# Two graph layers on one core: the relation loop's last two rounds peeled off, and the node arithmetic and h2 scatters of 47 groups placed in front of them

## The chip, the cores and the metric

The kernel runs on one core of a Trainium2 chip. The metric is the time of one execution on the device in microseconds, as the median of several. The engines of the core are TensorE (PE in the profile; PEld is its weight load), VectorE (DVE), ScalarE (ACT), GpSimd (POOL) and SyncE (SP). Each works through its own instruction list, and they meet at semaphores.

## The reference, cut to what matters

There are 6250 nodes with 16 features each, 206250 directed edges, and 230 relations. Two layers follow each other:

```
deg = max(number of edges that end in the node, 1);  h = relu(layernorm(x))
x  = x + L0(h, deg ** -0.5, rel_weight, loop_weight, rel_emb, src, dst, edge_type)
h  = relu(layernorm(x))
x  = x + L1(h, edge_attr, W_msg, b_msg, W_attn, b_attn, src, dst)
```

L0 (the relation layer) takes for each edge the row of its source node times the matrix of its relation, maps it with a tanh of its norm, weights it, and sums over the edges of each destination (`numer`, and the weights in `lamsum`). After the sums comes arithmetic per node: a division, a projection to a ball, an addition of the node's own transformed row, a residual sum (`xnew`), and then layernorm and relu of that, which gives `h` for the next layer, called h2 here. L1 (the edge layer) makes two 16 x 16 matrices for each edge from its 16 attributes, multiplies them with the h2 row of the edge's source, and takes a softmax-weighted sum over the edges of each destination.

## The kernel before

Edges come sorted by destination. The kernel ranks the nodes by their number of edges, largest first, and puts them into GC = 49 groups of 128 (one node in each partition). A round, also called a window, treats up to S = 48 edges of each of the 128 nodes of one group. The first group needs two windows, every other one, so there are 50 rounds, numbered k = 0 to 49; the loops run over pairs of rounds (25 iterations), q = k mod 2 chooses the buffer. The last two rounds, 48 and 49, are those of the last two groups, 47 and 48, which have the fewest edges: round 48 has 24 slots and round 49 has 22.

**Set-up.** All relation products go into a table in HBM (`table`), the nodes are ranked, the plan of the windows is made.

**Relation phase** (loop at L358 on POOL, L1022 on DVE, L669 on ACT). For each round POOL issues one indirect DMA per slot (L354, 128 rows of 16 numbers from `table` into `gath`): 18 in any case, then the indices of the next round (`pair_block`, L349), then the rest. DVE waits until all of the round's gathers have landed (L1033), does the arithmetic of the round (L1034 to L1057, with a Sqrt and a Tanh on ACT), and adds to `numer` and `lamsum` of the group. POOL may start the gathers of round k when DVE has finished round k-2 (`l0_math`, L363). In the same loop DVE turns the edge attributes into rows of 100 bf16 numbers, `split_chunk` (L1003 to L1014), one of 50 chunks in each round; SP writes each chunk to `ef6` in HBM (L281) and then loads the chunk after next into the same buffer (L278). The split of a chunk waits for its data, and for the write of the chunk two before it.

**Between the phases.** After the loop DVE does the node arithmetic for all 49 groups at once (L1071 to L1113): tiles of 128 x 784 numbers, one after another, with three square roots on ACT (L676 to L681), and signals `h2_ready`. POOL has waited meanwhile: it needs `start_ready` from ACT (L698), which comes after ACT's third square root. POOL then fetches the source numbers of the first edge window (`src_block`, L387), the edge rows of that window (`edge_rows`, L391, 128 rows of 4800 numbers), and the source numbers of the second, and writes the h2 rows of the 49 groups to HBM by 49 indirect DMAs (L402). It waits until all of these have landed (`h2_out`, L424).

**Edge phase.** 50 windows again. For each, POOL gathers up to 48 h2 rows per node (L354), TensorE transposes the edge rows (L551) and makes the matrices (L557), and DVE multiplies them with the gathered rows (L1182), takes maxima and products, TensorE sums. The first window's products wait for all of its gathers (L1177).

Work that POOL issues goes into one queue in the order of its instructions.

Of the kernel before, what the change touches and what calls it, by code (L numbers as in the profile page):

```python
# [10 lines left out]
ALU = mybir.AluOpType  # L11
# [18 lines left out]
GSTEP = 64  # L30
MINS = MINH * HALF
# [4 lines left out]
WCH = 512  # L36
# [23 lines left out]
def build(nc, x, src, dst, efeat, etype, relw, loopw, relemb, wmsg, bmsg, wattn, battn, out, scratch):  # L60
# [3 lines left out]
    with ctx:  # L64
# [64 lines left out]
        def col256(j, n=1):  # L129
# [71 lines left out]
                 "bst_ready blk_in tg0 tg1 l0_math n2_ready th_ready hnorm hnorm_out h2_ready h2_out "  # L201
# [11 lines left out]
        def steps(eng):  # L213
            n = eng.value_load(npair[0:1, 0:1], min_val=(GC + 1) // 2, max_val=NW // 2 - 2)
            return n, (2 * n + 2) // WCH + 1
# [82 lines left out]
        def _(pool):  # L298
# [38 lines left out]
            pairs = pool.value_load(npair[0:1, 0:1], min_val=(GC + 1) // 2, max_val=NW // 2 - 2)  # L337
# [18 lines left out]

            pair_block(0, 0)
            with pool.Fori(0, pairs) as i:  # L358
                for q in range(2):
                    k = 2 * i + q  # L360
                    _, ns = window_slots(pool, k)
                    pool.wait_ge(m["blk_in"], 16 * k + 16)
                    pool.wait_ge(m["l0_math"], k + 1)  # L363
                    pool.sem_inc(m["passed"], 1)
                    for b in range(MINS):
                        gather(table_d, blkidx, q, b, 1, tgath)
                    if q:
                        pool.wait_ge(tgath[0], pool.snap(cum[0]) * 16)
                        pool.sem_inc(m["passed"], 1)
                    else:  # L370
                        with pool.If(i > 0):
                            pool.wait_ge(tgath[1], pool.snap(cum[1]) * 16)
                            pool.sem_inc(m["passed"], 1)
                    pair_block(k + 1, 1 - q)
                    with ExitStack() as deeper:
                        for b in range(MINS, S):
                            deeper.enter_context(pool.If(ns > b))
                            gather(table_d, blkidx, q, b, 1, tgath)
                    pool.reg_add(cum[q], cum[q], ns)
            pool.wait_ge(m["blk_in"], pairs * 32 + 16)  # L380
            pool.sem_inc(m["passed"], 1)
# [107 lines left out]
        def _(pe):  # L489
# [43 lines left out]
            pairs, nstep = steps(pe)  # L533
# [93 lines left out]
        def _(act):  # L627
# [40 lines left out]
            pairs = act.value_load(npair[0:1, 0:1], min_val=(GC + 1) // 2, max_val=NW // 2 - 2)  # L668
            with act.Fori(0, pairs) as i:  # L669
                for q in range(2):  # L670
                    k = 2 * i + q
                    act.wait_ge(m["n2_ready"], k + 1)
                    nc.scalar.activation(sl[:, 2, :], sl[:, 1, :], ACT.Sqrt)  # L673
                    nc.scalar.drain()
                    nc.scalar.activation(sl[:, 3, :], sl[:, 2, :], ACT.Tanh, scale=SQC).then_inc(m["th_ready"], 1)
            act.wait_ge(m["hnorm"], 1)  # L676
            nc.scalar.activation(nrm[:, 1, 0:GC], nrm[:, 0, 0:GC], ACT.Sqrt).then_inc(m["hnorm_out"], 1)
            act.wait_ge(m["hnorm"], 2)
            nc.scalar.activation(nrm[:, 1, 0:GC], nrm[:, 0, 0:GC], ACT.Sqrt).then_inc(m["hnorm_out"], 1)
            act.wait_ge(m["hnorm"], 3)  # L680
            nc.scalar.activation(nrm[:, 1, 0:GC], nrm[:, 0, 0:GC], ACT.Sqrt).then_inc(m["hnorm_out"], 1)  # L681
# [73 lines left out]
        def _(dve):  # L755
# [188 lines left out]
            ts(npairf[:], npairf[:], -MAGIC, None, ALU.add)  # L944
# [18 lines left out]
            pairs, nstep = steps(dve)  # L963
# [58 lines left out]
            with dve.Fori(0, pairs) as i:  # L1022
                for q in range(2):
                    k = 2 * i + q
                    G = gath[:, q, :, :]
                    g, ns = window_slots(dve, k)
                    dve.reg_add(cum[q], cum[q], ns)
                    V.tensor_scalar(valid[:, q, :], iotaf[:, 0:S], rem[:, q:q + 1], None, ALU.is_lt)
                    V.drain()
                    dve.wait_ge(m["blk_in"], 16 * k + 16)  # L1030
                    dve.sem_inc(m["passed"], 1)
                    window_start(k + 2, q, m["bst_ready"])
                    dve.wait_ge(tgath[q], dve.snap(cum[q]) * 16)  # L1033
                    tt(sq, G, G, ALU.mult)  # L1034
                    row_sum(sl[:, 0, :], sq)
                    V.tensor_scalar(sl[:, 1, :], sl[:, 0, :], MIN_NORM, None, ALU.max).then_inc(m["n2_ready"], 1)  # L1036
                    dve.wait_ge(m["th_ready"], k + 1)
                    ts(sl[:, 2, :], sl[:, 2, :], SQC, None, ALU.mult)
                    V.reciprocal(sl[:, 4, :], sl[:, 2, :])
                    V.drain()  # L1040
                    tt(sl[:, 3, :], sl[:, 3, :], sl[:, 4, :], ALU.mult)
                    tt(sl[:, 4, :], sl[:, 3, :], sl[:, 3, :], ALU.mult)
                    tt(sl[:, 4, :], sl[:, 4, :], sl[:, 0, :], ALU.mult)
                    ts(sl[:, 4, :], sl[:, 4, :], -CURV, 1.0, ALU.mult, ALU.add)
                    ts(sl[:, 4, :], sl[:, 4, :], EPS, 0.5, ALU.add, ALU.mult)
                    V.reciprocal(sl[:, 5, :], sl[:, 4, :])
                    V.drain()
                    tt(sl[:, 5, :], sl[:, 5, :], valid[:, q, :], ALU.mult)
                    row_sum(lsum[:], sl[:, 5, :])
                    tt(sl[:, 3, :], sl[:, 3, :], sl[:, 5, :], ALU.mult)  # L1050
                    V.tensor_tensor(sq, G, bc(sl[:, 3, :], D), ALU.mult)
                    V.drain().then_inc(m["l0_math"], 1)
                    row_sum(nsum[:], sq.rearrange("p s d -> p d s"))
                    V.tensor_tensor(numer[:, ds(g, 1), :].rearrange("p a d -> p (a d)"),
                                    numer[:, ds(g, 1), :].rearrange("p a d -> p (a d)"), nsum[:], ALU.add)
                    V.tensor_tensor(lamsum[:, ds(g, 1)], lamsum[:, ds(g, 1)], lsum[:], ALU.add)
                    V.drain()  # L1057
# [6 lines left out]
            dve.wait_ge(m["blk_in"], pairs * 32 + 16)  # L1064
            dve.sem_inc(m["passed"], 1)


            A, B, T = gtmp(0), gtmp(1), gtmp(2)
            X0, Y = info[:, 0:GC, 0:D], info[:, 0:GC, D:2 * D]
            n0, n1, n2, n3, n4, n5 = (nrm[:, j, 0:GC] for j in (2, 3, 4, 5, 6, 7))  # L1070
            V.tensor_scalar(nrm[:, 0, 0:GC], deg[:, 0:GC], 1.0, None, ALU.max).then_inc(m["hnorm"], 1)  # L1071
            dve.wait_ge(m["hnorm_out"], 1)
            V.reciprocal(n0, nrm[:, 1, 0:GC])
            V.drain()
            tt(n1, n0, deg[:, 0:GC], ALU.mult)
            ts(n1, n1, EPS, None, ALU.add)
            V.reciprocal(n2, n1)
            V.drain()
            tt(n0, n0, n2, ALU.mult)
            tt(n1, n0, lamsum[:, 0:GC], ALU.mult)  # L1080
            ts(n1, n1, EPS, None, ALU.add)
            V.reciprocal(n2, n1)
            V.drain()
            tt(n0, n0, n2, ALU.mult)
            tt(A, numer[:, 0:GC, :], bc(n0, D), ALU.mult)
            tt(T, A, A, ALU.mult)
            row_sum(n0, T)
            V.tensor_scalar(nrm[:, 0, 0:GC], n0, MIN_NORM, None, ALU.max).then_inc(m["hnorm"], 1)
            dve.wait_ge(m["hnorm_out"], 2)
            V.reciprocal(n1, nrm[:, 1, 0:GC])  # L1090
            V.drain()
            ts(n1, n1, (1.0 - BALL) / SQC, 1.0, ALU.mult, ALU.min)
            tt(A, A, bc(n1, D), ALU.mult)
# [184 lines left out]
```

## Time and profile before

| | us |
|---|---|
| median of 3 runs | 6012.68 |
| lowest and highest of the runs | 6012.58, 6017.94 |
| span of the profiled execution | 6008.9 |
| VectorE busy (58% of the span) | 3466.2 |
| GpSimd busy (69%) | 4164.0 |
| TensorE busy (45%) | 2731.4 |

The profiled execution has no time of its own beside its span; the span runs from its first to its last instruction, and the median of the runs is 3.8 us longer. "Busy" says how long an engine worked, not whether anybody waited for it. The granted clock of TensorE is 0.50 of full speed while it idles in the relation phase and about 0.87 in the edge phase.

### The profile page before, as it was taken

Reading aid. Unit: us, or ns where it says so; the run is one execution under the profiler, and the core shown is the slowest. Engines: PE = TensorE matmul, PEld = TensorE weight load, DVE = VectorE, ACT = ScalarE, POOL = GpSimd, SP = SyncE. Lnnn points to the kernel's source line nnn. Section 1 sums busy time; section 2 is a strip of 40 time slices with the busy share of each in tenths; the row PEclk is TensorE's granted clock in tenths of the full one; section 3 lists DMA queues with packets and bytes.
Section 4 is the critical chain, followed back from the end, with each engine's and each line's share of the span. In section 5 each row is a group of like instructions: output and inputs, shape, how many; then the busy total and the mean of one; then the engine's idle time right before and its main releaser. Section 6 shows DMA issues by size and latency. Waiting matters only on the chain.

```text
span 6008.9 us, 57574 instructions
## 1 busy us (share of the span) xinstructions
PE 2731.4 (45%) x13577; PEld 1934.4 (32%) x13578; DVE 3466.2 (58%) x4171; ACT 1368.7 (23%) x1709; POOL 4164.0 (69%) x3713
## 2 busy tenths in 40 slices
PE   3550000000000000000678787888888888887887
PEld 1110000000000000000455565565565656555665
DVE  8601222222222322341688888888888888888886
ACT  3540000000000000000222233223323333333333
POOL 2326777777777777756476777777777777777774
PEclk6555555555555555555788889888888889888988
DMA  5881111111111111111000000100010101011110
GB/s 148 271 263 31 28 23 27 29 33 31 28 30 34 33 31 36 36 38 22 21 13 21 21 21 21 29 21 21 21 30 21 30 22 30 23 28 30 29 29 19
DMA packets 157959, 251.69 MB, mean 42 GB/s; under 512 B 73726, under 2 KB 130563, under 8 KB 145156
## 3 DMA queue, kind: packets, MB, share of 16 engines
q0 software_dynamic: 126192, 100.10, 8.5%
q1 hardware_dynamic: 31711, 151.31, 7.7%
q8 instruction: 9, 0.15, 0.0%
q14 instruction: 15, 0.12, 0.0%
q10 hardware_dynamic: 32, 0.01, 0.0%
HBM read 113.57 MB, written 136.63 MB: 42 GB/s over the span
## 4 chain that ended last, share of the span: by engine, by line
POOL 29%; PE 21%; issue 16%; DVEq 14%; DVE 12%; DMA 6%; POOLq 1%; ACT 1%; SPq 0%; ACTq 0%
POOL gath L354 28%; PE psS L563 9%; PE psS L568 7%; DVEq L1221 6%; DMA table<-arena 4%; DVE stage L1182 4%; PE psW L557 3%; DVE stage L1224 3%; DVEq L1189 2%; DVEq L1182 1%; DVE arena L1182 1%; DMA gath<-h_dram,hidx 1%; DVEq L1138 1%; PE psW L511 1%; DVEq L1151 1%
## 5 line engine op out<-in xcount | busy, mean ns | idle before, releaser
L354 POOL DMA_INDIRECT gath<-h_dram,hidx x1695 | 2100.0, 1239 | 798.9 <-issue 528.0
L354 POOL DMA_INDIRECT gath<-table,blkidx x1646 | 1641.4, 997 | 507.4 <-issue 504.5
L551 PE MATMUL psT<-identb,stage 128*100 128x128 bf16 x2448 | 225.7, 251 | 2341.4 <-DVEq L1138 2322.7
L568 PE MATMUL psS<-stage,ident 128*128 128x256 f32 x3390 | 926.7, 429 | 162.6 <-DVE stage L1224 161.8
L551 PEld LDWEIGHTS psT<-identb,stage 128*100 128x100 bf16 x2448 | 201.8, 150 | 2381.8 <-DVEq L1138 2280.5
L563 PE MATMUL psS<-arena,ident 128*128 128x256 f32 x3390 | 834.7, 384 | 0.0
L1182 DVE TENSOR_TENSOR arena<-psW,gath 128x768 f32 (+1 forms) x565 | 520.8, 951 | 494.4 <-DMA gath<-h_dram,hidx 363.4
L568 PEld LDWEIGHTS psS<-stage,ident 128*128 128x128 f32 x3390 | 703.5, 215 | 313.8 <-DVE stage L1224 205.1
L782 DVE TENSOR_TENSOR work<-gath 128x768 f32<-128x768 f32 x50 | 48.0, 959 | 1286.5 <-DMA gath<-table,blkidx 1286.5
L557 PE MATMUL psW<-wst,stage 100*128 100x256 bf16 x3390 | 576.8, 291 | 294.5 <-DVE arena L1182 212.2
L563 PEld LDWEIGHTS psS<-arena,ident 128*128 128x128 f32 x3390 | 608.5, 192 | 71.2
L712 ACT ACTIVATE arena<-arena 128x1536 f32<-128x1536 f32 (+1 forms) x294 | 421.4, 1433 | 893.2 <-DVE arena L1211 893.2
L1182 DVE TENSOR_TENSOR stage<-psW,gath 128x768 f32 (+1 forms) x565 | 513.7, 949 | 14.8 <-issue 14.8
L1224 DVE TENSOR_TENSOR stage<-stage,arena (+1 forms) x294 | 498.9, 1697 | 30.4 <-ACT arena L712 4.6
L1211 DVE TENSOR_TENSOR arena<-arena,psT 128x1536 f32 (+2 forms) x294 | 495.0, 1684 | 0.0
L673 ACT ACTIVATE work<-work 128x48 f32<-128x48 f32 x50 | 12.1, 243 | 2066.3 <-DVE work L1036 2066.3
L557 PEld LDWEIGHTS psW<-wst,stage 100*128 100x128 bf16 x3390 | 294.4, 101 | 576.4 <-DVE arena L1182 257.3
L707 ACT ACT_TABLE_LOAD x50 | 64.2, 1283 | 1092.7 <-PE psS L571 1092.7
L1196 DVE TENSOR_TENSOR work<-work,arena 128x1536 f32<-128x1536 f32 x171 | 300.7, 1759 | 15.8
L702 ACT COPY stage<-psT 100x1024 bf16<-100x1024 bf16 x306 | 300.7, 996 | 10.4 <-PE psT L551 10.4
L511 PE MATMUL psW<-stage,work 102*125 102x460 bf16 x400 | 181.6, 606 | 194.2 <-ACT arena L645 162.7
L645 ACT COPY arena<-psW 125x920 f32<-125x920 f32 x200 | 175.3, 927 | 211.3 <-DMA table<-arena 159.2
(227 smaller groups left out, 2394.6 us busy)
## 6 DMA issues: line engine op xcount, KB each, us to landing
table<-arena SPq DMA_DIRECT2D x50, 1610.0 KB
ef<-arena SPq DMA_DIRECT2D x50, 805.7 KB
gath<-h_dram,hidx POOLq DMA_INDIRECT x1695
gath<-table,blkidx POOLq DMA_INDIRECT x1646, 2.3
arena<-in_edge_attr SPq DMA_DIRECT2D x50, 257.8 KB
table<-arena SPq DMA_DIRECT2D x50, 186.9 KB
arena<-first_dram POOLq DMA_DIRECT2D x1, 915.5 KB, 12.0
info<-info_dram POOLq DMA_DIRECT2D x2, 432.0 KB, 11.3
```

Source lines behind the costliest of these rows:

```text
L354: pool.indirect_dma_start(out=gath[:, q, s, :], out_offset=None, in_=rows, in_offset=bass.IndirectOffsetOnAxis(ap=idx[:, q, s:s + 1].bitca ...
L551: last = nc.tensor.transpose(psTb[0:KE, t % 2, j, 0:GP], efs[:, 8 * t + j, :], identb[0:GP, 0:GP])
L557: last = nc.tensor.matmul(psW[0:GP, h % 2, j * IO:(j + 1) * IO], efT[:, q, h * HALF + j, 0:GP], wst[:, c0:c0 + IO], start=True, stop=True)
L563: nc.tensor.matmul(psS[0:GP, 0:IO], ident[0:GP, 0:GP], score[:, q, s, :], start=False, stop=False)
L568: nc.tensor.matmul(psS[0:GP, IO:2 * IO], ident[0:GP, 0:GP], prod[:, c0:c0 + IO], start=False, stop=False)
L702: nc.scalar.copy(efT[:, q, 8 * t:8 * t + 8, 0:GP], psTb[0:KE, t % 2, :, 0:GP]).then_inc(m["efT_sb"], 1)
L712: nc.scalar.activation(v, v, ACT.Exp).then_inc(m["exp_done"], 1)
L1182: V.tensor_tensor(dst_ap.rearrange("p s (i o) -> p s i o", o=D), psW[0:GP, s, 0:HALF * IO].rearrange("p (s i o) -> p s i o", i=D, o=D), bc ...
L1196: V.tensor_tensor(macc, macc, score[:, q, ds(b * BLK, BLK), :], ALU.max).then_inc(m["scored"], 1)
L1211: V.tensor_tensor(blk, blk, mnew.unsqueeze(1).to_broadcast([GP, n, IO]), ALU.subtract).then_inc(m["sub_done"], 1)
L1221: V.drain()
L1224: V.tensor_tensor(pr, pr, score[:, q, ds(b * BLK, n), :].rearrange("p s c -> p (s c)"), ALU.mult).then_inc(m["q_ready"], 1)
```

## The change

The loops of the relation phase run over one pair of rounds less (`rest` instead of `pairs`), and the last two rounds stand behind them as code of their own. On DVE, the two chunks that the last pair would have split are split right after the loop; then the node arithmetic is done for groups 0 to 46 (GE = 47), which signals `h2_early`; then rounds 48 and 49; then the node arithmetic of groups 47 and 48, which signals `h2_ready`. On ACT the square roots go in the same order. On POOL the gathers of rounds 48 and 49 come first as before; then it waits for `h2_early` and issues 47 of the h2 scatters; then come the waits for the last gathers and `start_ready`, the three fetches for the edge phase, the wait for `h2_ready`, and the last two scatters. One `pair_block`, that of a round 50 which nobody used, and the waits for it are gone.

```
-            with pool.Fori(0, pairs) as i:
+            with pool.Fori(0, rest) as i:
                 for q in range(2):
...
+                    table_rows(i, q, False)
+            for q in range(2):
+                table_rows(rest, q, True)
...
-            pool.wait_ge(m["start_ready"], 1)
-            src_block(0)
-            edge_rows(0)
-            pool.wait_ge(m["start_ready"], 2)
-            src_block(1)
-
-            pool.wait_ge(m["h2_ready"], 1)
+            pool.wait_ge(m["h2_early"], 1)
             for c in range(GC):
+                if c == GE:
+                    pool.wait_ge(tgath[1], pool.snap(cum[1]) * 16)
+                    pool.sem_inc(m["passed"], 1)
+                    pool.wait_ge(m["start_ready"], 1)
+                    src_block(0)
+                    edge_rows(0)
+                    pool.wait_ge(m["start_ready"], 2)
+                    src_block(1)
+                    pool.wait_ge(m["h2_ready"], 1)
                 pool.indirect_dma_start(out=h2_d, ...
...
+            with dve.If(rest < ECH // 2):
+                for q in range(2):
+                    dve.wait_ge(m[f"ef6_out{q}"], 16 * (ECH // 2 - 1))
+                    dve.sem_inc(m["passed"], 1)
+                    split_chunk(ECH // 2 - 1, q)
+            nodes(0, GE, 0, m["h2_early"])
+            for q in range(2):
+                relation(rest, q)
+            nodes(GE, GC, 3, m["h2_ready"])
```

`relation` and `nodes` are the bodies that stood in the loop (L1025 to L1057) and behind it (L1068 to L1114), with the range of groups a to b as arguments; the instructions are the same. The loop of the relation phase keeps its split of one chunk in each round, now for rounds 0 to 47.

How the instructions stand. First POOL before, from its last gathers of the relation phase on (`table` is where these read; `srcp` holds the source numbers, `ef` the edge rows, `h_dram` is h2 in HBM; ISA rows are waits and register work):

```order
L354 DMA gath<-table,blkidx 128x16
L375 UNCONDITIONAL_BRANCH
L379 ISA
L358 COMPARE_AND_BRANCH
L380 ISA
L387 DMA blkidx<-srcp,ebst 128x48
L391 DMA stage<-ef,ebst 128x4800
L387 DMA blkidx<-srcp,ebst 128x48
L402 DMA h_dram<-arena,nidx 6251x16 x49
```

POOL with the change, at the same place:

```order
L356 DMA gath<-table,blkidx 128x16
L379 UNCONDITIONAL_BRANCH
L383 REGISTER_ALU
L415 DMA h_dram<-arena,nidx 6251x16 x47
L407 ISA
L397 DMA blkidx<-srcp,ebst 128x48
L401 DMA stage<-ef,ebst 128x4800
L397 DMA blkidx<-srcp,ebst 128x48
L415 DMA h_dram<-arena,nidx 6251x16 x2
```

The three fetches stood between the last gather and all 49 scatters; now 47 scatters stand in front of them and 2 behind.

DVE before, at the end of the relation loop (the four rows on `arena` are the split of a chunk, the rows on `nrm` the start of the node arithmetic):

```order
L1006 CAST arena<-arena 125x33x48
L782 TENSOR_TENSOR arena<-arena 125x528
L1010 CAST arena<-arena 125x33x32
L1013 TENSOR_TENSOR arena<-arena 125x33x16
L1058 UNCONDITIONAL_BRANCH
L1022 REGISTER_ALU
L1022 COMPARE_AND_BRANCH
L1064 ISA
L1071 TENSOR_SCALAR nrm<-info 128x49
L1073 RECIPROCAL nrm<-nrm 128x49
L782 TENSOR_TENSOR nrm<-nrm,info 128x49
```

DVE with the change, behind the loop:

```order
L1025 CAST arena<-arena 125x33x48
L801 TENSOR_TENSOR arena<-arena 125x528
L1029 CAST arena<-arena 125x33x32
L1032 TENSOR_TENSOR arena<-arena 125x33x16
L1025 CAST arena<-arena 125x33x48
L801 TENSOR_TENSOR arena<-arena 125x528
L1029 CAST arena<-arena 125x33x32
L1032 TENSOR_TENSOR arena<-arena 125x33x16
L1135 UNCONDITIONAL_BRANCH
L1081 TENSOR_SCALAR nrm<-info 128x47
L1083 RECIPROCAL nrm<-nrm 128x47
```

The loop's end has moved ahead of two splits, and the node arithmetic behind them has 47 columns; the 49-column arithmetic is gone, and rounds 48 and 49 come later, behind the 47 columns.

## Rows read from the trace of the kernel before

**Rows 1.** The page's chain that ended last, shares by engine.

```profile
POOL 29%; PE 21%; issue 16%; DVEq 14%; DVE 12%; DMA 6%; POOLq 1%; ACT 1%; SPq 0%; ACTq 0%
```

**Rows 2.** Windows by phase: us, busy (x instructions) by engine, PEclk, DMA share, GB/s.

```profile
457.00:2686.00 2229.00, 0.00 (x0) 0.00 (x0) 574.50 (x1301) 152.57 (x200) 1689.67 (x1697) 0.50 0.13 31
...
2848.00:6009.00 3161.00, 2525.39 (x13008) 1855.58 (x13008) 2624.34 (x2561) 1011.27 (x1260) 2249.25 (x1796) 0.87 0.10 24
```

**Rows 3.** Timeline of POOL between the phases: start, length, instruction, idle before.

```profile
2663.59 0.94 POOL L349 DMA_INDIRECT blkidx<-pairp,bst  x1 [0.30 <-issue]
...
2668.58 0.94 POOL L354 DMA_INDIRECT gath<-table,blkidx  x1 [0.30 <-issue]
2716.69 0.94 POOL L387 DMA_INDIRECT blkidx<-srcp,ebst  x1 [47.17 <-ACTq L698]
2717.94 0.94 POOL L391 DMA_INDIRECT stage<-ef,ebst  x1 [0.30 <-issue]
...
2720.44 1.03 POOL L402 DMA_INDIRECT h_dram<-arena,nidx  x1 [0.30 <-issue]
...
2782.28 0.98 POOL L402 DMA_INDIRECT h_dram<-arena,nidx  x1 [0.30 <-issue]
2786.23 0.99 POOL L354 DMA_INDIRECT gath<-h_dram,hidx  x1 [2.97 <-issue]
```

**Rows 4.** Timeline of DVE, from the node arithmetic to the first edge window.

```profile
2685.90 0.20 DVE L1071 TENSOR_SCALAR nrm<-info 128x49 f32<-128x49 f32 x1 [0.47 <-issue]
...
2715.13 0.57 DVE L787 TENSOR_SCALAR arena<-arena 128x784 f32<-128x784 f32 x1
...
2723.84 0.33 DVE L1137 TENSOR_SCALAR stage<-iotaf,erem 128x48 bf16<-128x48 f32 x1 [4.09 <-DMA stage<-ef,ebst]
...
2847.73 1.82 DVE L1182 TENSOR_TENSOR arena<-psW,gath 128x768 f32<-128x768 f32 x2 [123.05 <-DMA gath<-h_dram,hidx]
```

**Rows 5.** Timeline of PE, between the phases.

```profile
2731.47 1.22 PE L557 MATMUL psW<-wst,stage 100*128 100x256 bf16 x6 [1.26 <-ACT stage L702]
```

**Rows 6.** Timeline of SP's queue, behind the split of round 47.

```profile
2623.35 0.28 SPq L281 DMA_DIRECT2D ef<-arena  x1
```

**Rows 7.** Windows behind that write, same columns as Rows 2.

```profile
2624.00:2626.00 2.00, 0.00 (x0) 0.00 (x0) 0.45 (x1) 0.00 (x0) 1.42 (x2) 0.50 0.33 102
...
2634.00:2636.00 2.00, 0.00 (x0) 0.00 (x0) 0.00 (x0) 0.00 (x0) 1.44 (x2) 0.50 0.12 19
```

**Rows 8.** Timeline of POOL during round 48 on DVE.

```profile
2640.50 1.62 POOL L354 DMA_INDIRECT gath<-table,blkidx  x1 [0.30 <-issue]
...
2648.65 1.21 POOL L354 DMA_INDIRECT gath<-table,blkidx  x1 [0.30 <-issue]
...
2651.42 1.28 POOL L354 DMA_INDIRECT gath<-table,blkidx  x1 [0.30 <-issue]
2653.00 1.29 POOL L354 DMA_INDIRECT gath<-table,blkidx  x1 [0.30 <-issue]
2654.60 1.21 POOL L354 DMA_INDIRECT gath<-table,blkidx  x1 [0.30 <-issue]
```

**Rows 9.** Timeline of DVE, rounds 47 to 49.

```profile
2622.45 0.71 DVE L1013 TENSOR_TENSOR arena<-arena 125x528 bf16<-125x528 f32 x1
...
2640.34 0.96 DVE L782 TENSOR_TENSOR work<-gath 128x768 f32<-128x768 f32 x1 [12.57 <-DMA gath<-table,blkidx]
...
2651.62 1.01 DVE L1006 CAST arena<-arena 125x1584 bf16<-125x1584 f32 x1 [0.51 <-issue]
...
2654.28 0.71 DVE L1013 TENSOR_TENSOR arena<-arena 125x528 bf16<-125x528 f32 x1
...
2670.86 0.96 DVE L782 TENSOR_TENSOR work<-gath 128x768 f32<-128x768 f32 x1 [12.19 <-DMA gath<-table,blkidx]
```

**Rows 10.** Groups of DVE by shape, node arithmetic: busy us, mean ns, idle before.

```profile
L782 DVE TENSOR_TENSOR arena<-arena 128x784 f32<-128x784 f32 x4 | 3.9, 977 | 0.3
...
L787 DVE TENSOR_SCALAR arena<-arena 128x784 f32<-128x784 f32 x1 | 0.6, 571 | 0.1
```

More of the change, by code:

```diff
@@ L30 @@
 GSTEP = 64
+GE = GC - 2
 MINS = MINH * HALF
@@ L200, in build @@
                  "passed tab_ready wraw_in wsplit win_iota loop_n loop_t "
-                 "bst_ready blk_in tg0 tg1 l0_math n2_ready th_ready hnorm hnorm_out h2_ready h2_out "
+                 "bst_ready blk_in tg0 tg1 l0_math n2_ready th_ready hnorm hnorm_out h2_early h2_ready h2_out "
                  "scored start_ready src_in0 src_in1 ef_in idx_ready valid_in mold_ready m0_ready "
@@ L213, in steps @@
         def steps(eng):
[L214 to L215 removed]
+            n = eng.value_load(npair[0:1, 0:1], min_val=(GC - 1) // 2, max_val=NW // 2 - 3)
+            return n, n + 1, (2 * n + 4) // WCH + 1
         def window(eng, k):
@@ L336, in _ @@
             pool.wait_ge(m["win_ready"], 16)
-            pairs = pool.value_load(npair[0:1, 0:1], min_val=(GC + 1) // 2, max_val=NW // 2 - 2)
+            rest = pool.value_load(npair[0:1, 0:1], min_val=(GC - 1) // 2, max_val=NW // 2 - 3)
+            pairs = rest + 1
             pool.wait_ge(m["tbl_out0"], 2 * 16 * (C // 2))
@@ L355, in gather, with table_rows @@
                                             in_offset=bass.IndirectOffsetOnAxis(ap=idx[:, q, s:s + 1].bitcast(U32), axis=0)).then_inc(done[q], 16)
+            def table_rows(i, q, last):
+                k = 2 * i + q
+                _, ns = window_slots(pool, k)
+                pool.wait_ge(m["blk_in"], 16 * k + 16)
+                pool.wait_ge(m["l0_math"], k + 1)
+                pool.sem_inc(m["passed"], 1)
+                for b in range(MINS):
+                    gather(table_d, blkidx, q, b, 1, tgath)
+                if q:
+                    pool.wait_ge(tgath[0], pool.snap(cum[0]) * 16)
+                    pool.sem_inc(m["passed"], 1)
+                elif last:
+                    pool.wait_ge(tgath[1], pool.snap(cum[1]) * 16)
+                    pool.sem_inc(m["passed"], 1)
+                else:
+                    with pool.If(i > 0):
+                        pool.wait_ge(tgath[1], pool.snap(cum[1]) * 16)
+                        pool.sem_inc(m["passed"], 1)
+                if not (last and q):
+                    pair_block(k + 1, 1 - q)
+                with ExitStack() as deeper:
+                    for b in range(MINS, S):
+                        deeper.enter_context(pool.If(ns > b))
+                        gather(table_d, blkidx, q, b, 1, tgath)
+                pool.reg_add(cum[q], cum[q], ns)
@@ L357, in _ @@
             pair_block(0, 0)
-            with pool.Fori(0, pairs) as i:
+            with pool.Fori(0, rest) as i:
                 for q in range(2):
[L360 to L379, printed above, removed]
@@ L667, in _, with slot_norms, node_norms @@
             act.wait_ge(m["win_ready"], 16)
-            pairs = act.value_load(npair[0:1, 0:1], min_val=(GC + 1) // 2, max_val=NW // 2 - 2)
-            with act.Fori(0, pairs) as i:
-                for q in range(2):
[L671 to L681, printed above, removed]
+            rest = act.value_load(npair[0:1, 0:1], min_val=(GC - 1) // 2, max_val=NW // 2 - 3)
+            pairs = rest + 1
+            def slot_norms(k):
+                act.wait_ge(m["n2_ready"], k + 1)
+                nc.scalar.activation(sl[:, 2, :], sl[:, 1, :], ACT.Sqrt)
+                nc.scalar.drain()
+                nc.scalar.activation(sl[:, 3, :], sl[:, 2, :], ACT.Tanh, scale=SQC).then_inc(m["th_ready"], 1)
+            def node_norms(a, b, n):
+                for j in range(1, 4):
+                    act.wait_ge(m["hnorm"], n + j)
+                    nc.scalar.activation(nrm[:, 1, a:b], nrm[:, 0, a:b], ACT.Sqrt).then_inc(m["hnorm_out"], 1)
+            with act.Fori(0, rest) as i:
+                for q in range(2):
+                    slot_norms(2 * i + q)
+            node_norms(0, GE, 0)
+            for q in range(2):
+                slot_norms(rest * 2 + q)
+            node_norms(GE, GC, 3)
             def edge_start(w, q):
@@ L962, in _ @@
             V.drain().then_inc(m["plan_col"], 1)
-            pairs, nstep = steps(dve)
+            rest, pairs, nstep = steps(dve)
             with dve.Fori(0, nstep) as t:
@@ L1058, in _ @@
+            with dve.Fori(0, rest) as i:
+                for q in range(2):
+                    relation(i, q)
                     with dve.If(i < ECH // 2):
@@ L1062, in _ @@
                         split_chunk(i, q)
[L1064 to L1087, printed above, removed]
@@ L1111, in _ @@
-            tt(T, T, bc(n5, D), ALU.mult)
-            tt(xnew[:, 0:GC, :], X0, T, ALU.add)
-            norm_relu(h2, xnew[:, 0:GC, :], gtmp(3), nrm[:, :, 0:GC], m["hnorm"], m["hnorm_out"], 3)
-            V.drain().then_inc(m["h2_ready"], 1)
+            with dve.If(rest < ECH // 2):
+                for q in range(2):
+                    dve.wait_ge(m[f"ef6_out{q}"], 16 * (ECH // 2 - 1))
+                    dve.sem_inc(m["passed"], 1)
+                    split_chunk(ECH // 2 - 1, q)
+            nodes(0, GE, 0, m["h2_early"])
@@ L1117, in _ @@
+            for q in range(2):
+                relation(rest, q)
+            nodes(GE, GC, 3, m["h2_ready"])
             V.memset(mnew, 0.0)
```

148 lines of the change are left out of this document (86 added, 62 removed).

## The prediction

> **What bounds the kernel now.** I read first the page's chain that ended last: POOL has 29% of it, PE 21%, and issue time another 16% [rows 1], so no single engine bounds the whole, and each stage has to be looked at alone. The windows by phase come next [rows 2]. From 457 to 2686 us POOL works 1690 us of 2229; its gathers last 0.94 us each with 0.30 us between them [rows 3], and DVE works only 575 us: this phase goes at POOL's pace. From 2848 us on, DVE is busy 2624 of 3161 us and PE 2525: another regime, in which the change alters no instruction. So what matters lies between the last gather of the relation phase and the first gather of the edge phase, and there I read the timelines of POOL and DVE side by side.
>
> POOL issues the last table gather at 2668.58 and is done with it at 2669.52. Then it stands idle for 47.17 us, until 2716.69, and the releaser is ACT's start_ready [rows 3]. In these 47 us DVE ends rounds 48 and 49 (it starts the arithmetic of round 49 at 2670.86 [rows 9]) and does the node arithmetic, from 2685.90 to 2715.70, 29.8 us [rows 4]. From 2716.69 POOL has 52 DMAs to issue, three fetches and 49 scatters; the scatters run from 2720.44 to 2782.28, which is 61.84/48 = 1.288 us each, and the first edge gather follows at 2786.23 [rows 3]. That makes 69.54 us from the first fetch to the first edge gather. All this time DVE has almost nothing to do: its first edge product starts at 2847.73, after 123.05 us of waiting for the gathers of h2 [rows 4]. PE had the first matrices ready by 2732.69 [rows 5], 115 us too early. So POOL's instruction stream is the critical path from 2640 to 2847 us, with one hole in it, and every microsecond by which its first edge gather comes earlier should come off the end.
>
> **The change part by part.** On POOL the hole is between its last table gather and its next DMA. With the change the next DMA is a scatter, which needs h2_early only.
>
> *When does h2_early come?* DVE ends the split of round 47 at 2623.16 [rows 9]. It then splits chunk 48, about 3.9 us (2651.62 to 2654.99 for the four operations, 0.5 us ahead of them [rows 9]). Chunk 49 is later: its buffer is loaded only after chunk 47 has been written, and that write is issued at 2623.35 [rows 6]. The traffic behind it runs at 102 GB/s in 2624 to 2626 and has fallen to 19 GB/s in 2634 to 2636 [rows 7], so write and load have landed by about 2635. This load had a whole round to land in; now DVE waits some 7 us for it. Its split ends at 2635 + 3.9 = 2638.9. The node arithmetic takes 29.8 us less 20 large operations of 2/49 of 0.98 us (0.8 us), 29 us: h2_early at about 2668.
>
> *When is POOL ready for it?* Round 48's arithmetic is moved out of the gathers, one split and the node arithmetic are moved into them, and one pair_block (0.94 + 0.30 = 1.25 us [rows 3]) is gone. DVE's work delays POOL, and that is the one cost here that has to be sized. While DVE did round 48 and its split, five gathers took 1.62, 1.21, 1.28, 1.29 and 1.21 us [rows 8] in place of 0.94, 1.91 us lost; they lie beside the multiplies on the gathered tile (0.96 us each, two in a round) and the four operations of the split (3.4 us) [rows 9]; the small operations and sums between show no long gather. So 5.3 us of large elementwise work cost POOL 1.91 us, a share of 0.36. The node arithmetic has 14 multiplies, additions and subtractions of 0.98 us (the row of four stands for them, seven further groups hold the other ten) and one of 0.57 [rows 10]: 14.3 us, times 47/49 is 13.7, times 0.36 is 4.9 us. The two multiplies of a round lost 0.68 + 0.27 = 0.95 us, the split 0.96. Nothing in this phase shows whole tiles of this kind back to back under POOL. Bounds: 0 us if the gathers slip between them, and 13.7 us if POOL stands still through each; I take 5, because the rows nearest to it are the same operations at 768 columns. So POOL ends its gathers at 2669.52 - 1.25 - 0.95 (round 48 gone) + 0.96 (split of chunk 49 come) + 5 = 2673.3. That is 5 us behind h2_early: the hole closes completely, with 5 us to spare.
>
> The Trainium skill bears on the size ("SBUF — State Buffer", section "SBUF: two separate sides"): VectorE and GpSimd share a port pair as an exclusive lock, taken by a VectorE operation in a two-port mode or with two SBUF inputs, and the loser is blocked for the whole operation. The trace agrees in kind, not in size: 5.3 us of such work cost 1.91. By the rule's full length the node arithmetic would cost 13.7 us, which is the bound above and a rival below.
>
> *Behind the gathers.* The same 52 DMAs follow in another order, 69.54 us up to the first edge gather. New is that rounds 48 and 49 now run on DVE beside the scatters: 2 x 0.95 = 1.9 us lost. The scatters read SBUF tiles as well as indices, and the only one beside any DVE work took 1.03 us in place of 0.98 [rows 3], so 0 to 4 us; I take 1.9. Does anything make POOL wait before the last two? DVE's rounds 48 and 49 take at most 18.3 us each (2640.34 to 2670.86 less a wait of 12.19 [rows 9], a split still in it), and the node arithmetic on two groups less than 29.8 us, about 15 with the large operations down to the small ones' length: h2_ready and start_ready by 2668 + 37 + 15 = 2720. The 47 scatters end at 2673 + 61 + 2 = 2736. Cover of 16 us. The two last scatters now stand right behind edge_rows in the queue, whose data took until 2723.84 to be used, 5.9 us after the issue at 2717.94 [rows 3, 4]; the last scatter is issued 3.8 us behind edge_rows and its landing is what the first edge gather waits for. The scatter after edge_rows can't land before it does: 0 to 1.5 us more, I take 0.3. The edge rows themselves, the transposes and the first matrices come later against the gathers: they needed 2732.69 - 2717.94 = 14.8 us from their issue [rows 3, 5], and the first window's gathers alone run 2847.73 - 2786.23 = 61.5 us [rows 3, 4]. They stay hidden.
>
> *The sum*, against POOL's own path: + 47.17 (the hole) + 1.25 (pair_block) - 0.96 (split of chunk 49) - 5.0 (node arithmetic beside gathers) - 0.95 (two rounds beside scatters for the one that was beside gathers: 1.9 - 0.95) - 0.3 (landing) = 41.2 us. The first edge gather would start at 2786.2 - 41.2 = 2745.0, the profiled span would be 6008.9 - 41.2 = 5967.7, and the median, 3.8 us above the span, 6012.7 - 41.2 = 5971.5 us.
>
> Code that runs only once (the peeled rounds) could cost fetches; the code behind the loop in before, met for the first time, shows 0.30 us between DMAs as in the loop [rows 3], so I put it at 0.
>
> **The rivals.**
>
> *A: the forecast,* 5971.5 us, chance 0.79. With the bounds of its terms (node arithmetic 2 to 8 us, scatters 0 to 4, landing 0 to 1.5) the gain is 37 to 46, so 5966 to 5976.
>
> *B: full lock.* POOL stands still through every large operation: 13.7 us for the nodes, 3.4 for the split of chunk 49, 1.9 for the added round: gain 47.17 + 1.25 - 19 - 0.3 = 29, 5984 us. Rows 8 and 9 speak against it, where the same kinds of operation cost 0.36 of their length; for it, that back-to-back tiles leave no room to slip in. Chance 0.08.
>
> *C: h2_early is late.* If chunk 49's load comes later or the peeled code is slower by more than the 5 us of slack, POOL waits for DVE and each further microsecond is lost. With 15 us of lateness the gain is 31, 5982 us. For it: a 7 us wait is new on DVE. Against: rates in rows 7. Chance 0.07.
>
> *D: the gain is given back in the edge phase,* or the first window was held by something else than its gathers; the time stays within 0.2%, 6012 us. Against: DVE's 123 us wait has the gathers as its releaser, and PE was ready 115 us early [rows 4, 5]. Chance 0.04.
>
> *E: slower.* POOL is stopped whenever DVE is busy, small operations too. DVE would work some 4 + 29 + 37 + 15 = 85 us beside POOL; the gain is 48.4 us, so the change turns into a loss when POOL loses more than 0.57 of DVE's time beside it; at all of it, 48.4 - 85 = -37, 6049 us. In rows 8 and 9 it lost 1.9 us in the 14.7 from 2640.3 to 2655.0, 0.13. Chance 0.02.
>
> **How the numbers follow.** The predicted time is A's, 5971.5. The three runs span 5.4 us, and the edge phase may fall into step a little otherwise, so A's own range of 5966 to 5976 holds about 0.65 in all. To leave out no more than 2 in 10 it has to reach up to B and C: 5964 to 5984. A measurement of this kernel can tell about 0.2%, 12 us, from no change. A, B and C are all faster by more: 0.94. D is the same: 0.04. E is slower: 0.02.
>
> **What would show it.** In the new trace: no idle of tens of us on POOL between its last table gather and the first scatter, and that scatter at about 2673; DVE's 47-column arithmetic starting about 2639 and ending about 2668, with a wait of about 7 us before the second split; gathers between 1.2 and 2.1 us in that stretch, some 5 us in all above 0.94; no wait before the fetches or the last two scatters; the first edge gather at about 2745 and DVE's first product at about 2806; the rest shifted as a block. The prediction is wrong if a wait for h2_early stands in POOL's timeline, if the gathers beside the node arithmetic lose over 8 us, or if the edge phase isn't 3161 us long as before.

## The result, and the profile after

The changed kernel takes 5973.0 us (median of 4 runs, 5969.9 to 5979.3) against 6015.3 us (4 runs, 6012.6 to 6019.2): ratio 0.9934, 95% interval 0.9922 to 0.9946. That is 42 us faster; 5971.5 was forecast.

The span of the profiled execution and the chain that ended last, from the page of the changed kernel:

```profile
span 5971.1 us, 57669 instructions
POOL 29%; PE 21%; issue 16%; DVEq 14%; DVE 11%; DMA 6%; POOLq 1%; ACT 1%; SPq 0%; ACTq 0%
```

The shares of the chain are those of before [rows 1], but for DVE's, which is 11% and was 12%. The time gained is 0.7% of the span and can't be read from such shares; it has to be looked for in the timelines. Line numbers have moved: L354 is now L356 (gathers), L402 is L415 (h2 scatters), L387 and L391 are L397 and L401 (the fetches), L1182 is L1211 (first edge product).

POOL of the changed kernel in order of time, as in [rows 3] and [rows 8]:

```profile
2637.26 1.67 POOL L356 DMA_INDIRECT gath<-table,blkidx  x1 [0.30 <-issue]
2639.23 1.30 POOL L356 DMA_INDIRECT gath<-table,blkidx  x1 [0.30 <-issue]
...
2644.58 1.61 POOL L356 DMA_INDIRECT gath<-table,blkidx  x1 [0.30 <-issue]
...
2649.00 1.54 POOL L356 DMA_INDIRECT gath<-table,blkidx  x1 [0.30 <-issue]
...
2673.25 0.94 POOL L356 DMA_INDIRECT gath<-table,blkidx  x1 [0.30 <-issue]
2674.50 1.24 POOL L415 DMA_INDIRECT h_dram<-arena,nidx  x1 [0.30 <-issue]
2676.05 1.00 POOL L415 DMA_INDIRECT h_dram<-arena,nidx  x1 [0.30 <-issue]
...
2734.04 0.98 POOL L415 DMA_INDIRECT h_dram<-arena,nidx  x1 [0.30 <-issue]
2735.33 0.99 POOL L397 DMA_INDIRECT blkidx<-srcp,ebst  x1 [0.31 <-issue]
2736.63 0.97 POOL L401 DMA_INDIRECT stage<-ef,ebst  x1 [0.30 <-issue]
...
2740.48 1.00 POOL L415 DMA_INDIRECT h_dram<-arena,nidx  x1 [0.30 <-issue]
2744.95 0.98 POOL L356 DMA_INDIRECT gath<-h_dram,hidx  x1 [3.48 <-issue]
```

The idle time between the last table gather (2673.25) and the first h2 scatter (2674.50) is the usual 0.30 us: the hole of 47.17 us is closed. None has opened ahead of the fetches or the last two scatters either. The wait for the landing of the last scatter has grown from 2.97 to 3.48 us, and the first scatter, beside the arithmetic of round 48, took 1.24 us in place of 1.03. The first four rows show the price: gathers of 1.67, 1.30, 1.61 and 1.54 us, where 0.94 is the rule.

DVE of the changed kernel, as in [rows 4] and [rows 9]:

```profile
2610.80 0.96 DVE L801 TENSOR_TENSOR work<-gath 128x768 f32<-128x768 f32 x1 [14.62 <-DMA gath<-table,blkidx]
...
2625.91 1.18 DVE L1025 CAST arena<-arena 125x1584 bf16<-125x1584 f32 x1 [0.46 <-issue]
...
2637.16 1.01 DVE L1025 CAST arena<-arena 125x1584 bf16<-125x1584 f32 x1 [7.69 <-DMA arena<-in_edge_attr]
...
2640.65 0.20 DVE L1081 TENSOR_SCALAR nrm<-info 128x47 f32<-128x47 f32 x1
...
2669.71 0.56 DVE L806 TENSOR_SCALAR arena<-arena 128x752 f32<-128x752 f32 x1
...
2673.88 0.96 DVE L801 TENSOR_TENSOR work<-gath 128x768 f32<-128x768 f32 x1 [0.21 <-issue]
...
2688.13 0.96 DVE L801 TENSOR_TENSOR work<-gath 128x768 f32<-128x768 f32 x1 [0.21 <-issue]
...
2710.70 0.18 DVE L806 TENSOR_SCALAR arena<-arena 128x32 f32<-128x32 f32 x1
...
2806.46 1.82 DVE L1211 TENSOR_TENSOR arena<-psW,gath 128x768 f32<-128x768 f32 x2 [62.91 <-DMA gath<-h_dram,hidx]
```

From top to bottom: the arithmetic of round 47; the split of chunk 48; the split of chunk 49 after a wait of 7.69 us for its data; the start and the last operation of the node arithmetic on 47 columns (h2_early at 2670.3); rounds 48 and 49, whose gathers had long landed; the last operation on the last two groups (h2_ready at 2710.9); the first edge product, which waited 62.91 us where it had waited 123.05.

Absolute times can't be compared directly: the arithmetic of round 47 starts at 2610.80 here and at 2608.51 before [rows 9], although nothing ahead of it has changed. I therefore count from that start, as in all that follows ("behind round 47"). The first edge gather comes 2744.95 - 2610.80 = 134.15 us behind it, and came 2786.23 - 2608.51 = 177.72 us behind it: 43.6 us less. The first edge product comes 195.66 us behind it and came 239.22 us behind it: also 43.6 us less. The span is only 37.8 us shorter, since round 47 came 2.3 us later and the stretch behind the first edge product was 3164.6 us long and not 3161.2.

### The profile page after: what moved, and what is told of

It is laid out like the page before. It is cut to its first block, busy times and chain, and to the rows that moved or that the text cites. A ratio compares the mean times of both kernels' runs of the same rounds, so it can differ in the third digit from the quotient of the medians.

```text
span 5971.1 us, 57669 instructions
## 1 busy us (share of the span) xinstructions
PE 2735.7 (46%) x13577; PEld 1936.4 (32%) x13578; DVE 3475.3 (58%) x4215; ACT 1369.7 (23%) x1712; POOL 4162.4 (70%) x3712
## 4 chain that ended last, share of the span: by engine, by line
POOL 29%; PE 21%; issue 16%; DVEq 14%; DVE 11%; DMA 6%; POOLq 1%; ACT 1%; SPq 0%; ACTq 0%
POOL gath L356 28%; PE psS L576 9%; DVEq L1250 7%; PE psS L581 6%; DMA table<-arena 4%; DVE stage L1211 4%; PE psW L570 3%; DVE stage L1253 3%; DVEq L1218 2%; DVEq L1211 1%; DVE arena L1211 1%; DMA gath<-h_dram,hidx 1%; PE psW L524 1%; DVEq L1180 1%; ACT arena L658 1%
## 5 line engine op out<-in xcount | busy, mean ns | idle before, releaser
L356 POOL DMA_INDIRECT gath<-h_dram,hidx x1695 | 2095.2, 1236 | 808.2 <-issue 528.1
L356 POOL DMA_INDIRECT gath<-table,blkidx x1646 | 1645.1, 999 | 507.5 <-issue 504.7
L1211 DVE TENSOR_TENSOR arena<-psW,gath 128x768 f32 (+1 forms) x565 | 521.4, 952 | 437.4 <-DMA gath<-h_dram,hidx 303.1
L1211 DVE TENSOR_TENSOR stage<-psW,gath 128x768 f32 (+1 forms) x565 | 514.1, 950 | 14.8 <-issue 14.8
```

Source lines behind the costliest of these rows:

```text
L356: pool.indirect_dma_start(out=gath[:, q, s, :], out_offset=None, in_=rows, in_offset=bass.IndirectOffsetOnAxis(ap=idx[:, q, s:s + 1].bitca ...
L1211: V.tensor_tensor(dst_ap.rearrange("p s (i o) -> p s i o", o=D), psW[0:GP, s, 0:HALF * IO].rearrange("p (s i o) -> p s i o", i=D, o=D), bc ...
```

## The experiments

Eight kernels, all but the first made from the changed one. Times behind round 47 in us; "rest" is the stretch from the first edge product to the end.

| kernel | last gather issued to first scatter: idle | first scatter | first edge gather | first edge product | rest | span |
|---|---|---|---|---|---|---|
| before | no scatter there | 111.9 | 177.7 | 239.2 | 3161.2 | 6008.9 |
| before again | no scatter there | 112.0 | 177.9 | 239.6 | 3163.4 | 6017.1 |
| changed | 0.30 | 63.7 | 134.2 | 195.7 | 3164.6 | 5971.1 |
| scatters late | 38.45 | 100.8 | 170.9 | 232.4 | 3165.2 | 6012.9 |
| nodes twice | 26.23 | 89.5 | 161.3 | 222.8 | 3165.0 | 5998.5 |
| splits behind nodes | 0.58 | 63.8 | 134.0 | 195.5 | 3162.1 | 5970.5 |
| PSUM operands | 0.30 | 62.3 | 133.3 | 195.0 | 3168.5 | 5974.1 |
| work beside scatters | 0.30 | 63.7 | 139.8 | 201.3 | 3165.7 | 5975.5 |
| fetches earlier | 0.30 | 62.6 | 132.5 | 194.0 | 3164.0 | 5968.9 |
| PSUM operands and fetches | 0.30 | 62.2 | 132.8 | 194.5 | 3168.6 | 5977.1 |

### The kernel before, profiled a second time

The file is that of before, unchanged.

> The kernel before, unchanged, for a second profile of it: how far the set-up and the edge phase repeat from one profiled execution to another. Theory (both vary by some 2 to 4 us by themselves): the arithmetic of round 47 starts within 3 us of 2608.5, the first edge product follows 239.2 us behind it within 0.5 us, and the stretch from there to the end is 3161 us within 4. Rival (the edge phase repeats to 1 us, so that the 3.4 us by which it is longer in the changed kernel belongs to the change): 3161.2 within 1 us.

The first edge product came 239.6 us behind round 47, within 0.4 us of the first profile: the stretch in question repeats well. Round 47 started at 2614.1, 5.6 us later than in the first profile, more than I had expected, and the rest was 3163.4 us, 2.2 us longer. So the ends of the program vary by some microseconds by themselves, and a single span says nothing about a difference of 2 us; 19 runs of this file on the same chip took 6011.3 to 6032.2 us. Counting from round 47 does.

### The scatters late, all else changed

```
             pool.wait_ge(m["h2_early"], 1)
+            pool.wait_ge(m["h2_ready"], 1)
             for c in range(GC):
```

> The changed kernel with one wait more: POOL waits for h2_ready, not only for h2_early, ahead of the first h2 scatter, so that all else of the change stays and the scatters alone come late again. Theory A (the gain is POOL's hole, filled with scatters): POOL stands idle from about 2674 us until h2_ready at about 2711, the first edge gather comes at about 2781 (2745 with the change), and the time is 5973 + 36 = 6009 us, 5 to 7 us below the kernel before. Rival (the gain comes from the peeled loop, the pair_block left out, or the node arithmetic moved off DVE's end): it stays near 5973 us.

6014.6 us against 6025.4 (medians on the same chip), ratio 0.9982 (0.9972 to 0.9992), which is 5 to 17 us faster than before. (The 6009 us expected counted from the 5973.0 of the result, against which the kernel before took 6015.3 us and not 6025.4.) The timeline of POOL at this place:

```profile
2676.66 0.94 POOL L356 DMA_INDIRECT gath<-table,blkidx  x1 [0.31 <-issue]
2716.05 1.03 POOL L416 DMA_INDIRECT h_dram<-arena,nidx  x1 [38.45 <-DVEq L1125]
```

The hole is back, 38.45 us long, with DVE's signal for the last two groups (L1125) as its releaser, and the first edge gather comes 36.8 us later than in the changed kernel, as expected. What is left of the gain without the early scatters is 177.7 - 170.9 = 6.8 us: POOL's first DMA behind the hole stands 100.8 us behind round 47, and stood 108.2 us behind it before, since DVE is done sooner; the longer wait for the landing takes about 0.5 us of this back. The rival is refuted as the main cause: five sixths of the gain come from the scatters that fill the hole.

### The node arithmetic twice

```
-            nodes(0, GE, 0, m["h2_early"])
+            nodes(0, GE, 0, m["passed"])
+            nodes(0, GE, 3, m["h2_early"])
```

(and three more square roots on ACT; the second pass writes the same values again)

> The node arithmetic of the 47 groups is done twice in a row on DVE, h2_early signalled after the second, so that it comes 29.6 us later. Theory A (the hole is closed with about 4 us to spare, 2670.3 against 2674.2 us in the trace of the changed kernel): the first 4 us cost nothing, then each microsecond of lateness counts, POOL shows one wait of about 26 us ahead of the first scatter, 5973 + 26 = 5999 us. Rival 1 (h2_early is what POOL already waits for, no time to spare): 5973 + 30 = 6003 us. Rival 2 (DVE isn't on the path at all): 5973 us.

6001.6 us, ratio 0.9967 (0.9956 to 0.9977). POOL:

```profile
2673.07 0.94 POOL L356 DMA_INDIRECT gath<-table,blkidx  x1 [0.30 <-issue]
2700.25 1.03 POOL L415 DMA_INDIRECT h_dram<-arena,nidx  x1 [26.23 <-DVEq L1125]
```

DVE, the last operation of either pass:

```profile
2669.53 0.55 DVE L807 TENSOR_SCALAR arena<-arena 128x752 f32<-128x752 f32 x1
...
2698.70 0.55 DVE L807 TENSOR_SCALAR arena<-arena 128x752 f32<-128x752 f32 x1
```

DVE's first pass ends at 2670.08 and its second at 2699.25, 29.17 us later. POOL waits 26.23 us, 25.93 more than the usual 0.30, so that 3.2 us of lateness cost nothing. Behind round 47 the first edge gather is 27.1 us later than in the changed kernel; 1.3 us of that are scatters that now met DVE's multiplies (two took 1.73 and 1.68 us). This measures the spare time that the changed kernel has, 3.2 us where 5 were forecast, and from where on lateness counts in full.

### The two splits behind the node arithmetic

```
-            with dve.If(rest < ECH // 2): ...   (both splits)
             nodes(0, GE, 0, m["h2_early"])
+            with dve.If(rest < ECH // 2): ...   (both splits)
```

> The splits of chunks 48 and 49 stand behind the node arithmetic of the 47 groups, not ahead of it, which takes DVE's 7.7 us wait for chunk 49 and two splits of 3.5 us out of the way of h2_early: it comes at about 2656 in place of 2670 us. Theory A: POOL's gathers end at 2674 as before, nothing is gained, first scatter and first edge gather stay where they are within 1 us (2674.5 and 2745, each as far behind the start of round 47 on DVE as in the changed kernel). Rival C (h2_early is late and POOL's start hangs on it): up to 4 us less.

One run: 5972.2 us. The last operation of the node arithmetic on DVE, and POOL at its first scatter:

```profile
2656.82 0.56 DVE L806 TENSOR_SCALAR arena<-arena 128x752 f32<-128x752 f32 x1
```

```profile
2675.20 0.94 POOL L356 DMA_INDIRECT gath<-table,blkidx  x1 [0.30 <-issue]
2676.73 1.03 POOL L415 DMA_INDIRECT h_dram<-arena,nidx  x1 [0.58 <-issue]
```

h2_early came at 2657.4, 44.5 us behind round 47 in place of 59.5, and the first scatter 63.8 us behind it in place of 63.7. 15 us more of spare time bring nothing, as expected from a start that hangs on POOL's gathers alone. DVE's wait of 7.7 us for chunk 49, new with the change, is thus harmless; here it is gone.

### PSUM operands in the node arithmetic

```
-                A, B, T = (gtmp(j)[:, a:b, :] for j in range(3))
+                A, B = (gtmp(j)[:, a:b, :] for j in range(2))
+                flat = psT[0:GP, :, :].rearrange("p a n -> p (a n)")
+                T = flat[:, 0:(b - a) * D].rearrange("p (c d) -> p c d", d=D)
+                p = [flat[:, 1024 + 64 * j:1024 + 64 * j + (b - a)] for j in range(5)]
...
-                tt(n0, n0, n2, ALU.mult)
-                tt(A, numer[:, a:b, :], bc(n0, D), ALU.mult)
+                tt(p[0], n0, n2, ALU.mult)
+                tt(A, numer[:, a:b, :], bc(p[0], D), ALU.mult)
```

(and so on for the other factors)

> In the node arithmetic the scale factors that are spread over 16 columns and one product tile stand in PSUM: of the 14 large two-input operations 9 then have only one input in SBUF and 5 still have two; their number and length stay about the same (two small copies more). Theory by the port lock (only operations with two SBUF inputs, or in a two-port mode, hold up the start of a gather): the gathers beside the node arithmetic lose about 1.3 to 2 us in place of 3.7, the first scatter comes about 2 us nearer to the start of round 47 on DVE than in the changed kernel (63.7 us). Rival (any large work of DVE slows POOL, wherever its operands are): the loss stays at 3.7 us.

One run: 5975.9 us. The gathers beside the node arithmetic lost 2.3 us (what each gather of over 1 us took beyond 0.94, summed); in the six kernels with the arithmetic as the change has it they lost 2.4, 2.7, 2.7, 3.7, 3.7 and 3.7 us. The size is thus between the theory and the rival, and by the sum alone the two can't be told apart. The single rows can do it. POOL:

```profile
2644.44 0.95 POOL L356 DMA_INDIRECT gath<-table,blkidx  x1 [0.31 <-issue]
...
2645.69 1.39 POOL L356 DMA_INDIRECT gath<-table,blkidx  x1 [0.30 <-issue]
...
2649.89 1.61 POOL L356 DMA_INDIRECT gath<-table,blkidx  x1 [0.30 <-issue]
2651.81 0.95 POOL L356 DMA_INDIRECT gath<-table,blkidx  x1 [0.30 <-issue]
...
2658.45 0.95 POOL L356 DMA_INDIRECT gath<-table,blkidx  x1 [0.30 <-issue]
```

DVE beside it (psT is in PSUM):

```profile
2644.31 0.94 DVE L801 TENSOR_TENSOR arena<-stage,psT 128x752 f32<-128x752 f32 x1
2645.32 0.95 DVE L801 TENSOR_TENSOR psT<-arena 128x752 f32<-128x752 f32 x1
...
2649.74 0.95 DVE L801 TENSOR_TENSOR psT<-arena 128x752 f32<-128x752 f32 x1
...
2651.78 1.01 DVE L801 TENSOR_TENSOR psT<-info 128x752 f32<-128x752 f32 x1
...
2657.79 0.95 DVE L801 TENSOR_TENSOR psT<-arena,psT 128x752 f32<-128x752 f32 x1
```

The gather of 2645.69 starts inside a multiply with both inputs in `arena` (2645.32 to 2646.27) and takes 1.39 us; that of 2649.89 starts 0.15 us into another of these and takes 1.61. Both end 0.81 us behind the end of the multiply in which they started. The gather of 2644.44 starts 0.13 us into a multiply of the same length that reads one input from PSUM (2644.31 to 2645.25) and takes its normal 0.95; so does that of 2658.45. All four gathers over 1.3 us beside the node arithmetic started inside one of the five operations with two SBUF inputs; five gathers started inside one of the nine others, and all took 0.94 or 0.95 us. The kernel with PSUM operands and earlier fetches shows four and five again. The gather of 2651.81 started 0.03 us behind the start of a product of `info` with itself and kept its 0.95 us, while that product took 1.01 us in place of 0.94: here it seems to have been DVE that waited.

### More work beside the scatters

```
+            for _ in range(15):
+                tt(gtmp(2)[:, 0:GE, :], gtmp(0)[:, 0:GE, :], gtmp(1)[:, 0:GE, :], ALU.mult)
             nodes(GE, GC, 3, m["h2_ready"])
```

> 15 more multiplies of 128 x 752 with two SBUF inputs on DVE between round 49 and the arithmetic of the last two groups, beside the h2 scatters; their result is not used. They take 15 us. Theory A (scatters are delayed as gathers are, with a share of 0.25 to 0.36 of such work): the 47 scatters take 3.8 to 5.4 us longer than in the changed kernel, h2_ready comes at 2726, 9 us ahead of the last two scatters, and no wait appears: first edge gather 4 to 5 us later. Rival 1 (scatters are not delayed): nothing moves. Rival 2 (full lock): 14 us later, and more if h2_ready becomes late.

One run: 5977.3 us. POOL, and DVE beside it (one row for the 15 multiplies):

```profile
2700.04 1.73 POOL L415 DMA_INDIRECT h_dram<-arena,nidx  x1 [0.30 <-issue]
2702.07 1.73 POOL L415 DMA_INDIRECT h_dram<-arena,nidx  x1 [0.30 <-issue]
...
2710.22 1.73 POOL L415 DMA_INDIRECT h_dram<-arena,nidx  x1 [0.31 <-issue]
2712.25 0.98 POOL L415 DMA_INDIRECT h_dram<-arena,nidx  x1 [0.30 <-issue]
```

```profile
2696.92 15.19 DVE L801 TENSOR_TENSOR arena<-arena 128x752 f32<-128x752 f32 x15
```

As long as the multiplies last, a scatter comes every 2.035 us, once in two multiplies (15.19/15 = 1.013 us each); it takes 1.73 us and not 0.98. All scatters together lost 5.4 us, 0.4 in the changed kernel, so 5.0 us for 14.1 us of multiplies (15 x 0.94): a share of 0.36. Scatters are delayed like gathers, and a scatter in step with back-to-back work is the worst case of this kernel; the full lock is refuted, which would have cost 14. The first edge gather came 5.7 us later; 0.7 of that is the wait for the landing (4.18 us), for which I have no cause.

### The fetches earlier

```
-                if c == GE:
+                if c == 38:
                     (the waits and the three fetches)
-                    pool.wait_ge(m["h2_ready"], 1)
+                if c == GE:
+                    pool.wait_ge(m["h2_ready"], 1)
```

> The three fetches for the edge phase come ahead of the 39th h2 scatter in place of the 48th, about 12 us earlier, with the same waits. Theory A: edge_rows no longer stands ahead of the last scatter in the queue, and the wait between the last scatter and the first edge gather goes from 3.48 back to 2.97 us; nothing else moves, 0.5 us. Rival (the matrices of the first edge window are late and the first product waits for them): the first product would come nearer to the first edge gather than 61.5 us.

One run: 5970.7 us. POOL:

```profile
2722.66 0.99 POOL L397 DMA_INDIRECT blkidx<-srcp,ebst  x1 [0.30 <-issue]
2723.95 0.97 POOL L401 DMA_INDIRECT stage<-ef,ebst  x1 [0.30 <-issue]
...
2739.40 0.98 POOL L416 DMA_INDIRECT h_dram<-arena,nidx  x1 [0.30 <-issue]
2743.41 0.99 POOL L356 DMA_INDIRECT gath<-h_dram,hidx  x1 [3.02 <-issue]
```

The last wait is 3.02 us, so the 0.5 us is back, and the first product still comes 61.5 us behind the first edge gather. Behind round 47 all of it is 1.6 us earlier; the other 1.1 us were gained ahead of the first scatter, where this kernel is the same as the changed one: gathers fell otherwise beside DVE's operations (2.7 us lost in place of 3.7).

### Both together

> PSUM operands in the node arithmetic and the earlier fetches together. Theory A: 2 + 0.5 us less than the changed kernel, about 5970 us, which this comparison can hardly tell from 5973; against the kernel before a ratio of 0.9930. In the trace the first edge gather comes 131.6 us behind the start of round 47 on DVE in place of 134.15. Rival: no nearer than 134.

5978.8 us, ratio 0.9927 to before on the same chip (0.9913 to 0.9940). The first edge gather came 132.8 us behind round 47, 1.4 us nearer and not the 2.5 expected. The interval covers the changed kernel's 0.9934, so no kernel here is shown to beat it.

## Why the prediction was right

**What bounds the stretch.** Right: POOL's stream of DMAs. With the scatters late the time went back by 37 of 44 us, and with 15 us more of spare time on DVE nothing came of it.

**When h2_early comes, and whether the hole closes.** Right: 59.5 us behind round 47, forecast 2668 - 2608.5 = 59.5. DVE waited 7.69 us for chunk 49, forecast about 7. POOL ended its gathers 63.4 us behind round 47 (2674.19 - 2610.80), forecast 64.8; the spare time was 3.9 us by the trace of the changed kernel (from DVE's last operation to the end of POOL's last gather) and 3.2 us by the doubled arithmetic, forecast 5.

**The terms of the sum.** Forecast and measured, in us:

| term | forecast | measured |
|---|---|---|
| hole and pair_block | +48.4 | +48.1 |
| split of chunk 49 beside gathers | -1.0 | -1.1 |
| node arithmetic beside gathers | -5.0 | -3.7 |
| round 48 no longer beside gathers | +0.95 | +0.95 |
| split of chunk 48 beside gathers, otherwise placed | 0 | +0.3 |
| rounds 48 and 49 beside scatters | -1.9 | -0.3 |
| landing of the last scatter | -0.3 | -0.5 |
| sum | 41.2 | 43.7 |

43.6 us were measured behind round 47. The first term counts the whole 47.17 us as gained, where the usual 0.30 us between two DMAs stays. That DVE's work in the node arithmetic and in rounds 48 and 49 holds up POOL's DMAs was right, the two sizes were too large, for a reason that the runs show: of these operations only one with two SBUF inputs holds up a DMA, one that starts inside it. In the node arithmetic such operations come at most five in a row and are broken by sums, in which a gather starts freely; and of the four large multiplies of the two rounds only the first met the start of a scatter for long (the one of 1.24 us at 2674.50). How many are met is a matter of how the two streams fall together: the same arithmetic cost 2.4 to 3.7 us from kernel to kernel. The share of 0.36 which I had from [rows 8, 9] came out again where operations with two SBUF inputs followed each other without a break, but that is a coincidence: in the rows the casts of the split had a part in it.

**What is behind the first edge gather.** Right: the matrices of the first window were ready long ahead of its gathers. PE of the changed kernel:

```profile
2750.70 1.46 PE L570 MATMUL psW<-wst,stage 100*128 100x256 bf16 x6 [1.19 <-ACT stage L721]
```

They were ready at 2752.2, 54 us before they were used.

**The number.** That 5973.0 us came within 1.5 us of the forecast 5971.5 is in part luck. Up to the first edge product the gain was 2.4 us larger than the forecast sum. In the profiled pair of executions the later start of round 47 (2.3 us) and the longer rest (3.4 us) took more than that back, and the fourth run of the kernel before raised its median from the 6012.7 from which the forecast counts to 6015.3.

**Slips in the working.** The range of 37 to 46 us doesn't follow from the bounds given: with every term at its worst (8, 4 and 1.5 us) the gain is 35, which is 5978 us. Round 48 wasn't among what DVE did while POOL stood idle: its split had ended at 2654.99 [rows 9]; the sum doesn't use this.

**The rivals.** B (full lock) is refuted by the work beside the scatters, 5 us where it asks for 14, and by the node arithmetic, 3.7 us where it asks for 13.7. C (h2_early late) was 3.2 us away from being true, and the doubled arithmetic shows what it costs. D and E fell with the result.

**What stays open.** The rest behind the first edge product was 3161.2 and 3163.4 us in two profiles of before, 3162.1 to 3165.7 in six kernels with the change's order, and 3168.5 and 3168.6 in the two with PSUM operands, whose edge phase has the same instructions. The prediction named an edge phase that isn't 3161 us long as a sign that it is wrong; with 3164.6 us here and 3163.4 us in the second profile of before, this sign can't decide anything. Part of the stretch varies by itself; whether the change gives back a microsecond or two there, and why the last two are longer, I haven't tried to settle.

## What to carry to other kernels

Ask of an idle stretch of the engine that sets the pace not who ends it, but which part of the awaited result its next instruction needs; here 47 of 49 scatters needed nothing of the last two rounds, and peeling these off turned a wait of 47 us into work. Then count how long the new signal may be late: 3.2 us were left here, and beyond them each microsecond costs one. And when two short streams are put beside each other, compare stretches from a common event ahead of the change, since spans of this kernel vary by more than the smaller terms.

## What the runs showed that I had not expected

An indirect DMA on POOL is held up only at its start by a DVE operation with two SBUF inputs, until about 0.8 us behind that operation's end, and not at all by one of the same length with an input in PSUM: 1.39 and 1.61 us against 0.95. A cast is different. In [rows 8, 9] the gather of 2651.42 had run for 0.20 us when the cast of 2651.62 began, and took 1.28 us, until just behind the cast's end. In the Trainium skill ("SBUF — State Buffer", section "SBUF: two separate sides") the shared port pair is held for the whole of such an operation, and a two-input operation blocks only GpSimd work that reads SBUF. The runs agree that it's the operands that decide, and add that a DMA already past its start isn't touched by a two-input operation: the scatters beside the 15 multiplies all ran their last 0.8 us beside a multiply.

The granted clock of TensorE in the relation phase, where it is idle, was at one of its two levels in some executions and at the other in others: from 600 to 2500 us, without a matmul, 0.50 (1.2 GHz) in the first profile of before and 1.00 (2.4 GHz) in the second. The means over the span were 0.702 and 0.923 in the two profiles of before, and 0.718 in that of the changed kernel. The time doesn't follow it: the changed kernel's four runs were 5972.9 (0.718), 5969.9 (0.937), 5973.1 (0.937) and 5979.3 us (0.720).
